# Mixer chain: the low part of the mixing matrix formed by GpSimd instead of VectorE, fourth in its order of a step

## What is computed

```
def step(carry, inp):
    z, xs = carry
    Bt, Ct, At, dtt, St, ut = inp
    bu = Bt[..., :, None] * ut[..., None, :]
    z = s * (z - d * a * xs + d * bu)
    xs = xs + d * z
    y = jnp.einsum('bhn,bhnp->bhp', Ct, xs)
    return ((z, xs), y)
...
gated = (y + D_skip[None, None, :, None] * u) * jax.nn.silu(gate).reshape(Bsz, T, N_HEADS, D_HEAD)
```

## Time and profile before

| what | value |
|---|---|
| median of 3 runs | 1820.72 us (1814.13 to 1826.43) |
| profiled execution | 1814.29 us, span 1812.5 us |
| TensorE busy (matmul), whole span | 1481.0 us, 82% |
| VectorE busy | 1311.4 us, 72% |
| ScalarE busy | 1052.1 us, 58% |
| GpSimd busy | 383.6 us, 21% |
| mean granted TensorE clock | 0.883 |

### The profile page before, as it was taken

How to read it: one execution, slowest core, us unless ns; L and a number is a source line. 1 busy time by engine, 2 the same in 40 slices (tenths; PEclk the granted TensorE clock), 3 DMA queues, 4 the chain that set the end, 5 groups by cost and what they waited for, 6 DMA issues and landing times. The chain is left out here.

```text
span 1812.5 us, 36735 instructions
## 1 busy us (share of the span) xinstructions
PE 1481.0 (82%) x14334; PEld 1115.6 (62%) x14334; DVE 1311.4 (72%) x2831; ACT 1052.1 (58%) x1872; POOL 383.6 (21%) x393
## 2 busy tenths in 40 slices
PE   5898996886359879899999755997297899999795
PEld 5888985785235567674444545997286544446474
DVE  5988895589839755648997556886556369994666
ACT  6998895432258726455898323664101548995555
POOL 0000000000436510127960104674000320000100
PEclk9999998687659999897999757999598879999898
DMA  5120001000000010004530182121200000000101
GB/s 141 27 64 22 19 2 35 14 1 4 1 7 2 2 33 1 14 2 137 179 107 2 45 250 57 60 63 45 70 1 14 1 1 2 2 2 1 34 1 36
DMA packets 52725, 67.97 MB, mean 38 GB/s; under 512 B 11511, under 2 KB 41465, under 8 KB 52554
## 3 DMA queue, kind: packets, MB, share of 16 engines
q1 hardware_dynamic: 46586, 50.74, 9.2%
q0 software_dynamic: 3840, 9.18, 1.7%
q10 hardware_dynamic: 2128, 5.71, 1.3%
HBM read 46.97 MB, written 18.65 MB: 36 GB/s over the span
## 5 line engine op out<-in xcount | busy, mean ns | idle before, releaser
L2022 DVE TENSOR_REDUCE att_max<-banks 104x1 f32<-104x512 f32 (+1 forms) x480 | 295.9, 682 | 9.2 <-PE banks L1936 5.0
L2057 ACT ACTIVATE att_p<-banks 104x514 f32<-104x514 f32 (+1 forms) x480 | 262.0, 599 | 33.4 <-PE banks L1981 22.5
L339 PE MATMUL banks<-tok_wT,feature_halves 128*128 128x192 f16 x2592 | 229.7, 249 | 22.8 <-DVE feature_halves L365 11.7
L339 PEld LDWEIGHTS banks<-tok_wT,feature_halves 128*128 128x128 f16 x2592 | 217.4, 99 | 32.0 <-DVE feature_halves L365 17.4
L1997 PE MATMUL banks<-att_p,att_v 104*32 104x257 f32 (+1 forms) x1920 | 159.6, 405 | 0.9 <-ACT att_p L2057 0.3
L1981 PE MATMUL banks<-att_q,att_kT 64*104 64x257 f16 (+1 forms) x960 | 156.0, 304 | 2.9 <-ACT att_p L2057 2.5
L1936 PE MATMUL banks<-att_kT,att_q 64*104 64x512 f16 (+1 forms) x480 | 126.4, 424 | 4.6 <-DVE att_max L2022 2.1
L134 PE MATMUL banks<-ones 128*128 128x256 f16 x594 | 82.1, 296 | 56.7 <-PEq L113 26.6
L365 DVE TENSOR_TENSOR feature_halves<-features,feature_halves 128x2048 f16<-128x2048 f32 x54 | 123.3, 2283 | 6.2 <-ACT feature_halves L462 6.2
L1981 PEld LDWEIGHTS banks<-att_q,att_kT 64*104 64x104 f16 (+1 forms) x960 | 61.9, 123 | 106.7 <-ACT att_p L2057 79.4
L462 ACT CAST feature_halves<-features 128x2048 f16<-128x2048 f32 x54 | 102.2, 1893 | 11.0 <-PE banks L339 10.2
(11 more groups left out here) (464 smaller groups left out, 3421.2 us busy)
## 6 DMA issues: line engine op xcount, KB each, us to landing
expert_w_in<-in_L_ffn_w_dram SPq DMA_DIRECT2D x16, 576.0 KB, 4.6
expert_w_halves<-expert_w_halves SPq DMA_DIRECT2D x32, 288.0 KB, 2.3
tok_w<-in_L_tok_W_dram ACTq DMA_DIRECT2D x4, 1152.0 KB, 7.4
expert_w2s<-expert_w_halves SPq DMA_DIRECT2D x1, 4608.0 KB
expert_y<-expert_out SPq DMA_DIRECT2D x6, 513.0 KB
expert_w1s<-expert_w_halves SPq DMA_DIRECT2D x2, 1536.0 KB
raw<-in_x_dram SPq DMA_DIRECT2D x2, 1152.0 KB, 5.7
expert_w1s<-expert_w_halves SPq DMA_DIRECT2D x3, 768.0 KB
```

What stands on the lines that cost most here:

```text
L339: ins = pe.matmul(c.bank[t // 2][:, (t % 2) * D:(t % 2 + 1) * D], fh[:, s, q, z, t * 128:(t + 1) * 128], wT[:, y, k, 6 * q + wf, :], start ...
L2022: dve.reduce_max(mx[0:qn, n // NS % 2, 2 * gi + e, k:k + 1], bank_of(unit)[0:qn, 0:KEYS], X).then_inc(maxed, 1)
L2057: act.activation(p[0:kn, n % 4, :, :], c.pair[2 + n % 2][0:kn, :].rearrange("p (e q) -> p e q", e=2)[:, :, 0:HALF], ACT.Exp, scale=scale). ...
```

## The change

GpSimd gets `low_part`, as the fourth operation of its step (for n-1, behind the transition). It waits for both casts of that step and, from the third on, for the y products that last read that buffer of `wl`. VectorE loses it, and its `matrix` gets one more wait: `wt` may be written again only when the low part that reads it is done.

```diff
+            def low_part(n):
+                pool.wait_ge(wt_high, 2 * (n + 1))
+                if n >= 2:
+                    pool.wait_ge(y_done, n - 1)
+                pool.tensor_tensor(wl[0:L, n % 2, :, :], wt[:, n % 2, :, :], wh[0:L, n % 2, :, :], ALU.subtract
+                                   ).then_inc(wt_low, 1)
+                pool.wait_ge(wt_low, n + 1)
+
             for n, (ch, b, bc_) in enumerate(steps):
...
                 if 1 <= n <= last:
                     transition(n - 1)
+                if n:
+                    if n == 1:
+                        pool.wait_ge(padded, 2)
+                    low_part(n - 1)
+            low_part(N - 1)
             for n in (N - 3, N - 2, N - 1):
                 gate(n)
...
                 if n >= 2:
                     dve.wait_ge(wt_high, 2 * (n - 1))
+                    dve.wait_ge(wt_low, n - 1)
                 dve.tensor_tensor(wt[:, n % 2, :, :],
...
-            def low_part(n):
-                dve.wait_ge(wt_high, 2 * (n + 1))
-                dve.tensor_tensor(wl[0:L, n % 2, :, :], wt[:, n % 2, :, :], wh[0:L, n % 2, :, :], ALU.subtract
-                                  ).then_inc(wt_low, 1)
-
             dve.wait_ge(padded, 2)
             matrix(0)
             u_low_part(0)
             matrix(1)
-            low_part(0)
...
-                if n + 1 < N:
-                    low_part(n + 1)
                 dve.wait_ge(y_done, n + 1)
```

## The result

| | median | range | runs |
|---|---|---|---|
| before | 1819.08 us | 1808.09 to 1828.41 | 20 |
| after | 1824.63 us | 1822.27 to 1837.9 | 20 |

The ratio is 1.004, with a 95% interval of 1.0021 to 1.0059: 4 to 11 us slower. The profiled execution after has a span of 1823.1 us, against 1812.5.

What follows compares the result with a forecast made beforehand. Before, VectorE and a loop through its low_part bound the chain at 2.535 us a step; after, GpSimd's queue of 2.75. Start +2.1, middle +6.0, end +0.3 sum to +8.4 us: 1829 us from 1820.7, range 1818 to 1840.

Steps and rivals of the forecast that it cites:

- The price of the subtraction on GpSimd: Mixer chain, GpSimd: each added 57x342 subtraction takes 0.84 us, undisturbed by VectorE.
- Rivals 1 (0.68): GpSimd's subtraction at the low end, 0.68 us: queue 2.59 us, +4 us, 1825 us; chance 0.14.
- 2 (up to 1.16): GpSimd's reads held up, subtraction 0.95 to 1.16 us: at 1.16 queue 3.07, +18 us, 1839 us; chance 0.10.
- the estimate of 1.0 us: GpSimd's subtraction by the skill page's 1.96 times VectorE's 0.51 us: 1.0 us, sum about +13 us, 1834 us.
- GpSimd's queue of 2.75 us: Each chain step: GpSimd's four operations start to start take 2.75 us, above the 2.535 us step, and become the bound.
- GpSimd's wait ahead of the gate gone, TensorE waiting 0.4 us for C_by_head, VectorE busy 12 us of 20: Signs expected in the chain's profile after; GpSimd's wait before was 0.76 us a step.
- The two-step loop of 5.19 us: C_by_head through y products, matrix, casts and low part to the C_by_head after next: 2.60 us a step, under the queue.
- The start of 2.1 us: Chain's first steps: low_part(0) and low_part(2) wait for casts ahead of C_by_head, delaying step 4's C_by_head by 2.1 us.
- TensorE's slower clock: Rival: TensorE idles longer and its clock falls, possibly at the start: 1849 us for nine steps, 1880 for all; chance 0.04.
- the prediction's own walk: Start of the chain followed operation by operation: C_by_head of step 4 at 545.93 us, against 543.80 before.
- The end of 0.3 us: Chain from step 33 on: the two-step loop sets the pace and the last gate ends at 637.5 us; +0.3 us.
- "TensorE by itself would take about 2.36 us a step": Chain step before: 2.53 us less TensorE's 0.17 us wait for u_halves, so removing low_part gains up to 0.17 us.

Runs made afterwards that it cites:

- e1: Kernel before, with GpSimd also forming the same subtraction, fourth in its step, into a tile nobody reads: ratio 1.0124, 3.015 us a step.
- e2: Kernel after, with 30 of GpSimd's transitions left out, shortening its queue by 0.42 us: ratio 1.0005, 2.550 us a step.
- e5: Kernel after, with the low part second in GpSimd's step, behind C_by_head, ahead of gate and transition: ratio 1.0123, 3.135 us a step.
- e4: Kernel after, with the low part first in GpSimd's step, ahead of C_by_head, from step 3 on: ratio 1.064, 5.945 us a step.
- e8: Kernel after, with 14 more filler matmuls on TensorE in step 0, ahead of its wait for C_by_head: ratio 1.0081, stage 0.67 us shorter.
- e3: Kernel before, with GpSimd's transition issued ahead of its gate: ratio 0.9947, 2.226 us a step.
- e6: Kernel after, with the low part of step 0 formed by VectorE as before: ratio 1.0044, 2.786 us a step.
- e7: Kernel after, with the low part shared, heads 0 to 2 on GpSimd, 3 to 5 on VectorE: ratio 1.0004, 2.531 us a step.

## Why the prediction was right, point by point

- *The price of the subtraction on GpSimd*, 0.84 us from a line through 768 and 3456 elements: 0.829 measured, 0.824 to 0.833 in all 36 steps. Rivals 1 (0.68) and 2 (up to 1.16) are out, and the estimate of 1.0 us was too high: against VectorE's 0.51 us the ratio is 0.829 / 0.51 = 1.63. That no VectorE operation with two SBUF inputs was left, and so none to hold GpSimd up, is what e1 confirms from the other side: with VectorE's subtraction back, C_by_head takes 0.91 us.
- *GpSimd's queue of 2.75 us*: 2.765. Its parts are in the rows too, and there is no wait between them. e2 shows that it is the bound: with 0.42 us less in the queue the step falls, and as far as the loop. Middle: 6.44 us against 6.0.
- *GpSimd's wait ahead of the gate gone, TensorE waiting 0.4 us for C_by_head, VectorE busy 12 us of 20*: gone, 0.35 us and 11.73 us.
- *The two-step loop of 5.19 us*: 5.03 by the rows after (the y addition 1.48 us behind the fillers, not 1.6; the rows that the 1.6 was read from add up to 1.54), 5.10 in e2. That it lies under the queue was right. What I did not say is that it holds only in fourth place: whatever stands behind the low part in GpSimd's step is a link of the loop (e5), and ahead of C_by_head it closes in one step (e4).
- *The start of 2.1 us*: 2.75. The term was too small by 0.65 us. I had put TensorE's slower clock down as a rival with 0.04 and named the start as the place where it could happen; it did. TensorE idled 1.73 us there, the granted clock read 0.57 from 542 to 546 (1.00 before the change), and the y addition of step 0 came 2.05 us behind the fillers. e8 takes this away and gets 15.66 us, where the prediction's own walk had 545.93 - 530.23 = 15.70; that the two are so near is in part luck, since the walk's 1.6 us to the y addition is 0.12 too long and its first low part starts about 0.1 too early. The sign that was named for this rival, a clock below 1.00 from 545 to 620, reads 0.99 after the change: 0.59 from 545 to 546, which is the start again, and 1.00 from 546 on. So in the middle the rival failed. The Trainium skill's page "TensorE: Matmul & The Clock Gate", section "What's actually happening", says that the array's clock is set by how busy TensorE has lately been, between 1.2 and 2.4 GHz; the rows agree.
- *The end of 0.3 us*: the prediction has 0.2 of it in the step from 32 to 33; from 32 to the last gate it is 0.05 in the trace, as the prediction's two-step loop there was a little too long.
- *Sum*: 8.4 us forecast, 9.24 in the stage. Median 1829 forecast, 1824.6 measured: the base of three runs was 1.6 us higher than that of twenty, and the medians lie 5.5 us apart where the profiled executions lie 10.6 apart. The ratio's interval, 4 to 11 us, holds both the 8.4 and the 9.24; more the runs can't tell.
- *"TensorE by itself would take about 2.36 us a step"* was wrong. I took the waits that the profile names from the step, but an engine that is paced by others has slack between its own rows too. e3 runs at 2.226 us. It did not touch the forecast, since GpSimd's 2.75 lay above either, but it made the worth of removing the low part from VectorE 0.17 us a step where e3, which only shortens it, gives 0.31, and it is why e3 surprised me.

## What to carry to other kernels

Before work goes to an engine with spare time, add up that engine's queue start to start: GpSimd's 0.76 us free in each step were less than the 0.91 it was given. Ask too whether the operation to be moved is long or only held up: of VectorE's 0.83 us, 0.32 were waiting for GpSimd, and swapping two of GpSimd's operations gave 10 us where moving the work lost 7. In an order written by hand, count over how many steps a loop closes and what stands behind the moved operation: the same instruction in first, second and fourth place gave steps of 5.9 us (0.9 of it through the lower clock), 3.1 and 2.77 us.

## What the runs showed of the hardware

- A VectorE operation with two SBUF inputs and a GpSimd operation that reads SBUF hold each other up while they overlap, and the one that starts second is the longer: 0.83 against 0.51 us on VectorE, 0.91 against 0.76 (e1) and 0.60 against 0.35 (e3) on GpSimd. What is free is to choose who waits.
- One idle stretch of 1.73 us on TensorE, between stretches of work, came with a granted clock of 0.57 over the next 4 us. Fourteen fillers in it kept the clock at 1.00. In e6 the idle stretch was 1.56 us and the clock 0.50 from 544 to 548; in e7 it was 1.46 us and the clock 0.50 from 540 to 544.
- The same 39 filler matmuls at the head of the stage took 6.17 us in one execution and 5.48 in another, with granted clocks of 0.70 and 0.80: a difference of 0.7 us between two profiles can be that alone.
